# Expert stage of a convolution and attention network: tiles of 128 tokens, chunks of 256 and a last chunk of 64

## The reference, cut to what matters

```python
def _L2_ffn_ref(x, norm_w, wq, keys, expert_down, expert_up):
    HEADS = 8; DIM_KEY = 32; K = 16; NUM_KEYS = 64
    ...
    q = (x_norm @ wq).reshape(B, T, HEADS, 2, DIM_KEY)
    sim = jnp.einsum('bthpd,hkpd->pbthk', q, keys)
    s1, i1 = jax.lax.top_k(sim[0], K)
    s2, i2 = jax.lax.top_k(sim[1], K)
    all_idx = (i1[..., :, None] * NUM_KEYS + i2[..., None, :]).reshape(B, T, HEADS, K * K)
    all_scores = (s1[..., :, None] + s2[..., None, :]).reshape(B, T, HEADS, K * K)
    final_scores, pk = jax.lax.top_k(all_scores, K)
    final_idx = jnp.take_along_axis(all_idx, pk, axis=-1)
    wd = expert_down[final_idx]
    wu = expert_up[final_idx]
    hidden = jnp.einsum('btd,bthkd->bthk', x_norm, wd)
    hidden = jax.nn.gelu(hidden, approximate=False)
    hidden = hidden * jax.nn.relu(final_scores)
    return jnp.einsum('bthk,bthkd->btd', hidden, wu)
```

## Time and profile before

| | before |
|---|---|
| median of 3 executions | 2701.39 us |
| profiled execution, its own time | 2689.78 us |
| its span | 2688.1 us |
| PE busy, PEld busy | 2236.6, 1940.0 us |
| DVE busy | 1847.0 us |
| ACT, POOL busy | 663.9, 435.8 us |
| mean granted clock of TensorE | 0.82 of full speed |
| all data moved by DMA | 107.85 MB |

### The profile page before, as it was taken

The page is one execution under the profiler, slowest core; times in us unless marked ns, Lnnn a source line. Parts: engine busy times, 40 slices in busy tenths (PEclk is TensorE's granted clock), DMA queues, the critical chain, the costliest instruction groups (busy, mean ns, idle before and its releaser), DMA issues. The chain is left out here.

```text
span 2688.1 us, 50156 instructions
## 1 busy us (share of the span) xinstructions
PE 2236.6 (83%) x18017; PEld 1940.0 (72%) x18017; DVE 1847.0 (69%) x7732; ACT 663.9 (25%) x1527; POOL 435.8 (16%) x521
## 2 busy tenths in 40 slices
PE   6585999955989889989989889989888799648994
PEld 3464788734889788888989889889888577326663
DVE  4334666448889889898898898898895577440003
ACT  1432455432211111211211211111111255402220
POOL 2003444310101201102102012012012310030003
PEclk8777999966788697787787887887786799869996
DMA  1104444225000000000000000000000233042323
GB/s 53 34 18 98 106 108 99 47 73 118 5 4 1 5 5 2 5 5 2 5 1 5 5 1 5 5 1 5 1 1 1 65 83 81 7 165 82 104 92 102
DMA packets 87043, 107.85 MB, mean 40 GB/s; under 512 B 26222, under 2 KB 75502, under 8 KB 86062
## 3 DMA queue, kind: packets, MB, share of 16 engines
q1 hardware_dynamic: 81328, 96.62, 13.7%
q0 software_dynamic: 3296, 6.43, 0.9%
q10 hardware_dynamic: 2176, 1.61, 0.2%
HBM read 70.61 MB, written 30.51 MB: 38 GB/s over the span
## 5 line engine op out<-in xcount | busy, mean ns | idle before, releaser
L1540 PE MATMUL peer_x_ps<-peer_oh_h,peer_oh_a 128*128 128x32 bf16 x3136 | 417.2, 249 | 6.1 <-DVE peer_oh_l L1812 4.4
L1540 PEld LDWEIGHTS peer_x_ps<-peer_oh_h,peer_oh_a 128*128 128x128 bf16 x3136 | 414.2, 149 | 8.5 <-DVE peer_oh_l L1812 5.7
L1541 PE MATMUL peer_x_ps<-peer_oh_l,peer_oh_a 128*128 128x32 bf16 x3136 | 417.8, 249 | 0.0
L1541 PEld LDWEIGHTS peer_x_ps<-peer_oh_l,peer_oh_a 128*128 128x128 bf16 x3136 | 412.9, 149 | 3.6 <-issue 1.5
L1516 PE MATMUL peer_x_ps<-peer_xc,peer_dt 128*128 128x224 f32 x1792 | 374.4, 373 | 31.7 <-DMA peer_up<-in_L_ffn_expert_up_dram 19.4
L1482 POOL TENSOR_TENSOR peer_g<-peer_g,peer_qt 128x448 f32<-128x448 f32 x112 | 189.7, 1715 | 1275.0 <-ACT peer_qt L1639 1274.9
L1550 PE MATMUL peer_out_ps<-peer_g,peer_up 128*128 128x224 f32 x1792 | 370.9, 372 | 30.6 <-issue 28.4
L1516 PEld LDWEIGHTS peer_x_ps<-peer_xc,peer_dt 128*128 128x128 f32 x1792 | 362.1, 204 | 40.0 <-issue 34.6
L1550 PEld LDWEIGHTS peer_out_ps<-peer_g,peer_up 128*128 128x128 f32 x1792 | 361.1, 203 | 37.6 <-issue 32.4
L1617 ACT ACTIVATE peer_g<-peer_x_ps 128x448 f32<-128x448 f32 x224 | 121.9, 544 | 652.1 <-PE peer_x_ps L1516 652.1
L1277 DVE TENSOR_REDUCE l_attn_mx<-l_attn_s_ps 98x4 f32<-98x392 f32 (+1 forms) x320 | 175.0, 560 | 140.4 <-PE l_attn_s_ps L1047 100.6
(11 more groups left out here) (308 smaller groups left out, 3633.5 us busy)
## 6 DMA issues: line engine op xcount, KB each, us to landing
moe_w<-in_L_ffn_w_dram SPq DMA_DIRECT2D x16, 1024.0 KB, 9.1
l_attn_pieces_q_dram<-l_attn_pieces_q SPq DMA_DIRECT2D x16, 294.0 KB, 3.9
l_attn_pieces_k_dram<-l_attn_pieces_k SPq DMA_DIRECT2D x16, 294.0 KB, 3.1
l_attn_stq<-l_attn_pieces_q_dram SPq DMA_DIRECT2D x16, 294.0 KB
l_attn_stk<-l_attn_pieces_k_dram SPq DMA_DIRECT2D x16, 294.0 KB
peer_g<-n_L_ffn_expert_down_dram SPq DMA_DIRECT2D x8, 512.0 KB, 6.7
peer_up<-in_L_ffn_expert_up_dram SPq DMA_DIRECT2D x2, 2048.0 KB
l_xi<-net_x SPq DMA_DIRECT2D x16, 196.0 KB, 2.3
```

Source lines behind the costliest of these rows:

```text
L1540: nc.tensor.matmul(x_ps[q][:, i * J:(i + 1) * J], oh_a[hb % 2][:, :, t], oh_h[hb % 2][:, :, t], start=True, stop=False)
L1541: mm = nc.tensor.matmul(x_ps[q][:, i * J:(i + 1) * J], oh_a[hb % 2][:, :, t], oh_l[hb % 2][:, :, t], start=False, stop=True)
```

## The change

`TT` becomes 128 and with it `CT` 256, `HT` 64 and `GT` 16. 3136 tokens are 12 chunks of 256 and a rest of 64, half a tile. Every helper gets the number of tokens (`cols`, `rows`, `now`) as an argument; the rest is a thirteenth chunk with one tile, one quarter and 8 of the 16 lists in the second selection. The hardware loop now covers chunks 2 to 9; 10, 11 and the rest are written out behind it. SyncE gets one more load, of 64 tokens. Eleven intermediates of `make_codes` lose their own space and are put behind the tables in the `oh_a` buffers; for that the wait for `m_done` moves from L1749 to the top of `make_codes`, ahead of the candidate sums. Elements per partition of the steps in `make_codes` and `top_halves` stay what they were.

```diff
-    TT = 112
+    TT = 128
...
+    REST = NT - NCHUNK * CT
+    assert REST == HT
...
-        i16f, step16 = S.sb("i16f", [TT, NTILE * G16, TOP]), S.sb("step16", [TT, 2, TOP, HH], BF16)
...
-        sel = [oh_a[p][0:TT, :, :].rearrange("t r k -> t (r k)")[:, 0:TOP * PP].rearrange("t (a k) -> t a k", a=TOP) for p in range(2)]
+        flat = [oh_a[p][0:TT, :, :].rearrange("t r k -> t (r k)") for p in range(2)]
+        sel = [flat[p][:, 0:TOP * PP].rearrange("t (a k) -> t a k", a=TOP) for p in range(2)]
+
+        def behind(p, word, words, dt):
+
+            o = TOP * PP + 2 * word
+            return flat[p][:, o:o + 2 * words].bitcast(dt)
+
+        t1, t2, t3 = (behind(0, i * PP, PP, F32) for i in range(3))
+        bits, col = behind(0, 3 * PP, PP, U32), behind(0, 4 * PP, PP, U32)
...
             for p in range(2):
-                chunk(NCHUNK - 2 + p, p, p == 1)
+                chunk(NCHUNK - 2 + p, p, CT, CT if p == 0 else REST)
+            chunk(NCHUNK, 0, REST, 0)
+
+        def tile_rows(tokens):
+
+            return [min(TT, tokens - t0) for t0 in range(0, tokens, TT)]
...
             steps(sp, NCHUNK // 2 - 1, body)
+            sp.wait_ge(h_done, NPAIR * (NCHUNK - 1))
+            sp.dma_start(xc[0][:, :, 0:REST], xn_dram[:, :, NCHUNK * CT:NT].rearrange("k p t -> p k t")).then_inc(xc_in[0], 16)
...
-                            mm = nc.tensor.matmul(x_ps[b][:, jj * CT:(jj + 1) * CT], dt[:, k, 2 * jp + jj, :], xc[p][:, k, :],
+                            mm = nc.tensor.matmul(x_ps[b][:, jj * CT:jj * CT + cols], dt[:, k, 2 * jp + jj, :], xc[p][:, k, 0:cols],
...
-            def chunk(n, p, last):
-                hidden(n, p, range(EARLY))
-                for t in range(NTILE):
-                    turn(n, t)
-                hidden(n, p, range(EARLY, NPAIR))
-                if not last:
-                    queries(n + 1, 1 - p)
-                for hb in range(NHB):
+            def chunk(n, p, now, then):
+                hidden(n, p, range(EARLY), now)
+                for t, rows in enumerate(tile_rows(now)):
+                    turn(n, t, rows)
+                hidden(n, p, range(EARLY, NPAIR), now)
+                if then > 0:
+                    queries(n + 1, 1 - p, then)
+                next_rows = tile_rows(then)
+                for hb in range(now // HT):
                     scatter(n, hb)
-                    if hb < NTILE and not last:
-                        scores(n + 1, hb)
-                experts_out(n)
+                    if hb < len(next_rows):
+                        scores(n + 1, hb, next_rows[hb])
+                experts_out(n, now)
...
-            def make_codes(n):
-
+            def make_codes(n, tiles):
+
+                heads, rows = len(tiles) * NH, tiles[0]
                 v = v16[:, :, :].rearrange("t (h w) a -> t w h a", w=2)
                 o = 0
                 chain.wait()
+                wait(dve, m_done, 4 * NHB * n)
...
-                top16(f16, p16, [cv[:, h, :] for h in range(HH)])
+                top16(f16[0:rows, 0:heads, :], p16[0:rows, 0:heads, :], [cv[0:rows, h, :] for h in range(heads)])
...
-                wait(dve, m_done, 4 * NHB * n)
...
-            def chunk(n, p, last):
-                if p == 0:
+            def chunk(n, p, now, then):
+                if p == 0 and now == CT:
                     chain.turn(n, 2)
...
-                for hb in range(NHB - 1):
-                    one_hots(n, hb + 1)
+                for hb in range(n_hb):
+                    if hb + 1 < n_hb:
+                        one_hots(n, hb + 1)
                     if hb < LATE:
                         weigh(n, hb)
-                if not last:
-                    for t in range(NTILE):
-                        top_halves(n + 1, t)
-                    make_codes(n + 1)
+                if then > 0:
+                    for t, rows in enumerate(tile_rows(then)):
+                        top_halves(n + 1, t, rows)
+                    make_codes(n + 1, tile_rows(then))
                 dve.wait_ge(out_done, n + 1)
-                xs = x[:, :, bass.ds(n * CT, CT)]
+                xs = x[:, :, bass.ds(n * CT, now)]
```

More of the change, by code:

```diff
@@ L1474, in _ @@
             nc.gpsimd.memset(keys_b[:, :, :], 0.0).then_inc(iota_done, 1)
-            def chunk(n, p, last):
-                for hb in range(LATE, NHB):
+            def chunk(n, p, now, then):
+                for hb in range(LATE, now // HT):
                     for q in range(4):
@@ L1502, in scores, with hidden @@
                 for m in range(4):
-                    mm = nc.tensor.matmul(sim_ps[m // 2][0:TT, (m % 2) * 4 * NK:(m % 2 + 1) * 4 * NK], qt[:, m, t * TT:(t + 1) * TT],
+                    mm = nc.tensor.matmul(sim_ps[m // 2][0:rows, (m % 2) * 4 * NK:(m % 2 + 1) * 4 * NK], qt[:, m, t * TT:t * TT + rows],
                                           keys_b[:, m, :], start=True, stop=True)
                 mm.then_inc(sim_done, 1)
-            def hidden(n, p, pairs):
+            def hidden(n, p, pairs, cols):
                 for jp in pairs:
@@ L1558, in _ @@
             pe.wait_ge(keys_ready, 1)
-            queries(0, 0)
+            queries(0, 0, CT)
             for t in range(NTILE):
-                scores(0, t)
+                scores(0, t, TT)
             for s in range(J // JS):
@@ L1618, in hidden_out, with chunk @@
                                          ACT.Gelu).then_inc(gelu_done, 1)
-            def chunk(n, p, last):
+            def chunk(n, p, now, then):
                 wait(act, out_done, n)
-                hidden_out(n, range(EARLY))
-                for t in range(NTILE):
+                hidden_out(n, range(EARLY), now)
+                for t, rows in enumerate(tile_rows(now)):
                     act.wait_ge(tr_done, NTILE * n + t + 1)
-                    ts = slice(t * TT, (t + 1) * TT)
+                    ts = slice(t * TT, t * TT + rows)
@@ L1636, in chunk @@
-                for k in range(4 * (NHB - LATE)):
+                    nc.scalar.activation(wh_t[:, ts], tr_ps[:, 2 * TT:2 * TT + rows], ACT.Copy)
+                    nc.scalar.activation(a_t[:, ts], tr_ps[:, 0:rows], ACT.Copy)
+                    nc.scalar.activation(b_t[:, ts], tr_ps[:, TT:TT + rows], ACT.Copy).then_inc(tr_ready, 1)
+                hidden_out(n, range(EARLY, NPAIR), now)
+                if then > 0:
+                    query_out(n + 1, then)
+                    for t, rows in enumerate(tile_rows(then)):
+                        score_out(n + 1, t, rows)
@@ L1637, in chunk @@
+                for k in range(4 * max(0, now // HT - LATE)):
                     act.wait_ge(m_done, 4 * NHB * n + 4 * LATE + k + 1)
@@ L1702, in fold, with top_halves @@
                 else:
-                    chain.step(nc.vector.tensor_tensor(out[:, :], m[:, 0, :], m[:, 1, :], ALU.add))
-            def top_halves(n, t):
+                    chain.step(nc.vector.tensor_tensor(out, m[:, 0, :], m[:, 1, :], ALU.add))
+            def top_halves(n, t, rows):
                 dve.wait_ge(sim_ready, NTILE * n + t + 1)
@@ L1823, in _, with chunk @@
             for t in range(NTILE):
-                top_halves(0, t)
-            make_codes(0)
-            def chunk(n, p, last):
-                if p == 0:
+                top_halves(0, t, TT)
+            make_codes(0, tile_rows(CT))
+            def chunk(n, p, now, then):
+                if p == 0 and now == CT:
                     chain.turn(n, 2)
-                low_weights(n, 0)
+                tiles, n_hb = tile_rows(now), now // HT
+                low_weights(n, 0, tiles[0])
                 one_hots(n, 0)
-                low_weights(n, 1)
-                for hb in range(NHB - 1):
-                    one_hots(n, hb + 1)
+                if len(tiles) > 1:
+                    low_weights(n, 1, tiles[1])
+                for hb in range(n_hb):
+                    if hb + 1 < n_hb:
+                        one_hots(n, hb + 1)
                     if hb < LATE:
                         weigh(n, hb)
-                if not last:
-                    for t in range(NTILE):
-                        top_halves(n + 1, t)
-                    make_codes(n + 1)
+                if then > 0:
+                    for t, rows in enumerate(tile_rows(then)):
+                        top_halves(n + 1, t, rows)
+                    make_codes(n + 1, tile_rows(then))
                 dve.wait_ge(out_done, n + 1)
-                xs = x[:, :, bass.ds(n * CT, CT)]
-                nc.vector.tensor_tensor(xs, xs, out_ps[:, 0:KC * CT].rearrange("p (k t) -> p k t", k=KC), ALU.add).then_inc(x_done, 1)
+                xs = x[:, :, bass.ds(n * CT, now)]
+                nc.vector.tensor_tensor(xs, xs, out_ps[:, 0:KC * CT].rearrange("p (k t) -> p k t", k=KC)[:, :, 0:now], ALU.add).then_inc(x_done, 1)
             chunks(dve, chunk)
```

98 lines of the change are left out of this document (47 added, 51 removed).

## The result

The changed kernel takes **2795.36 us** (median of 4 runs, 2789.94 to 2806.3), the one before 2699.99 on the same chip (4 runs, 2695.79 to 2703.5): a ratio of 1.037, 95% interval 1.034 to 1.039. 2598 was forecast, with 0.04 for slower. The profiled execution took 2789.94 us, its span is 2788.2.

The account below looks back on a forecast made before the run. VectorE, in a loop through TensorE, was taken as the bound. First scatter 693.3 + intervals 1184.7 + last chunk 114.1 = 1992.1 us stage end, -103.0: 2586.8 profiled, plus 11.6 gives 2598 us; range 2575 to 2642.

Parts of the forecast that it names:

- What grows by 8/7 in a full chunk: Token-dependent work on VectorE's path per full chunk: scatters 0 and 1 14.7 to 16.8 us, one-hots 8.3 to 9.2.
- PE's sum: TensorE's own time per full chunk: 105.2 us, with scatters 33.7, some 2 us behind VectorE's path.
- Slower: the scatter's operands: Scatter matmuls reading one-hots at 128 bytes fetch slower; 16 ns more each eats the gain, up to 2955 us; chance 0.05.
- The fixed part: VectorE's selection and codes stay 60.1 us per chunk on 128 partitions, 11 times between chunks instead of 13.
- No gain: the fixed part isn't fixed: Selection and codes on VectorE grow by 8/7, 60.1 to 68.7 us, giving 2693 us; chance 0.03.
- The interval: Time between first scatters of successive full chunks: 107.7 us mean, 11 times, 1184.7 us, VectorE the bound by a hair.
- TensorE takes over: Low clock makes TensorE bound the chunks, mean 110 us, +25, 2623 us; chance 0.20 shared with the costly last chunk.
- POOL beside the one-hots: In a full chunk, POOL's products may hold a second VectorE one-hot instruction for 0 to 1.3 us; 1.0 taken.
- The start: Before the chunk loop: longer first hidden pairs move the first scatter from 690.01 to 693.3 us.
- The last chunk: The final 64 tokens: 114.1 us from the preceding chunk's scatter 0 to the stage's end, narrow hidden and output records at 120 ns.
- Dear tail: In the 64-token chunk, 208 narrow records cost 230 ns each: +23, 2621 us; chance 0.20 shared with TensorE bounding.
- The moved wait: VectorE's wait for all the chunk's scatters, ahead of the code steps: no waiting time, cost 0.

Follow-up runs that it names:

- the repaired kernel: Changed kernel with rows of all three one-hot buffers 136 bytes apart instead of 128, codes sharing the space of v16 and i16: 2597.63 us, ratio 0.961 to before.
- the fourth experiment: Kernel before (tiles of 112), one-hot rows in buffer 1 at 128 bytes, buffer 0 at 112, codes in the space of v16 and i16: 2747.5 us, one run.

## Why the prediction was wrong, step by step

- **The step that failed** is "What grows by 8/7 in a full chunk. Scatters 0 and 1: 14.7 to 16.8", and with it "scatters ... 33.7" in PE's sum. It took 66 ns per matmul over into a layout with another step. Measured: 2 x 12.6 = 25.2, and about 50 for four. In place of it stands the rival "Slower: the scatter's operands", mechanism and price: break-even was put at 16 ns more per matmul, and 32 more came (98 against 66): 6272 x 32 ns = 201 us against a gain of 103 makes +98, measured +100.1 in the span. All matmuls lie on the path because TensorE became the bound: VectorE waits 13 us in the chunk shown.
- **Its chance** of 0.05 rested on two sentences. "Both steps are far apart in memory" is true and beside the point: 32 bytes is near and 136 farther, and both are good. "Nothing in the trace depends on a step" was no evidence against: the trace of before has one single step, 112 bytes, for these loads, so it could not show a dependence. That argument speaks for a wide bound, such as this part asked of unknown costs everywhere else, and the range left the bound out.
- **The fixed part** held: 60.2 us for 60.1, on 128 partitions. Sixteen MAX8 take 2.16 us (1079.87 to 1082.03; 2.12 in the earlier trace rows), and the 128x2048 product 1215 to 1217 where 1223 was worked out. "No gain: the fixed part isn't fixed" is refuted.
- **The interval.** With the scatter repaired (136 bytes) it is (1859.05 - 681.89) / 11 = 107.0 us, forecast 107.7. But the bound is mostly the other engine than I had "by a hair": in nine of twelve chunks TensorE reaches the first turn without a wait, in three it waits 0.8 to 1.7 us for the codes, where 1 to 2 were forecast for all. By its rows: scatters and scores 40.5, POOL's last product 2.4, output 29.9, ten pairs 17.3, turns 2.1, six pairs and queries 13.8 = 106.0, and in three chunks the pause at a loop start, 2.1 to 2.9. The forecast for TensorE was 105.2. The low clock that the idling had caused left the pairs, as forecast: 10.53 us for 48 matmuls with 256 columns, where the earlier trace rows has 10.49 with 224. The rival "TensorE takes over" had the right engine and a mean that its own terms don't give: eight intervals of 108.1 and three of 110.7 make 108.8, not 110, so +12 and not +25. TensorE took over at 107.0.
- **POOL beside the one-hots**: one instruction of a chunk is held, as before: the last product of the fourth set takes 2.65 us in the repaired kernel at 1029.90, all others 1.22 or 1.23. The second hold, for which 1.0 us was added, is there in two chunks (the first, and the set at 1674.17) and missing in nine; in the last full chunk three are held, see the last chunk below. In the chunk of the changed kernel shown above there is none at all: its last set ends at 1079.95, and POOL's first product starts at 1078.90 and takes the delay itself (2.60 us).
- **The start**: from the first hidden product to the first scatter 32.5 us before, 34.9 after; +3.3 was forecast, +2.4 came.
- **The last chunk** was mis-sized: 128.4 us in the repaired kernel instead of 114.1. Hidden with 64 columns took 9.0 us for 80 records (113 ns; 120 taken), the output product 27.57 for 128, **215 ns each** instead of 120: +12.2. The stretches above show why: hidden runs at a granted clock of 1.00 (2.4 GHz), the output product at 0.50 (1.2 GHz) from its first microsecond to its last, with TensorE busy throughout; behind the wait of 3.4 us for the one-hots and the scatter the clock doesn't come back before the stage ends. The sum had 1.7 us for low clock. So the upper bound of 230 ns was the right price for 128 of the 208 records, a good half of the rival "Dear tail" (+23). The one-hots for the fourth scatter of the chunk before came 4.3 us late, too, a wait that the sum of TensorE's times left out. Three instructions of that set are held beside POOL, for 3.9 us together (DVE, then PE):

```profile
1884.57 2.63 DVE L1833 TENSOR_TENSOR peer_oh_l<-peer_b_t,peer_iota_f 128x2048 bf16<-128x2048 bf16 x1
1887.23 2.45 DVE L1836 TENSOR_TENSOR peer_oh_h<-peer_oh_l,peer_wh_t 128x2048 bf16<-128x2048 bf16 x1
1889.61 2.51 DVE L1836 TENSOR_TENSOR peer_oh_l<-peer_oh_l,peer_wl_t 128x2048 bf16<-128x2048 bf16 x1
```

```profile
1892.17 0.27 PE L1561 MATMUL peer_x_ps<-peer_oh_h,peer_oh_a 128*128 128x32 bf16 x1 [4.25 <-DVE peer_oh_l L1836]
```

- **The 2597.6 of the repaired kernel against 2598** is better than its terms, and luck. Against the forecast for a profiled execution the first scatter came 11.4 us earlier (681.89 for 693.3), the intervals took 7.5 less, the last chunk 14.3 more and what follows 15.1 more, +10.5 together; and of the 11.6 that were added to get from the profiled execution to the median, 0.3 came.
- **The moved wait, and the temporaries in the one-hot buffers**, taken at nothing: between the set's last product and the selection no wait is to be seen, and ahead of the codes the changed kernel has 0.2 us in the whole stage. No run undoes them by themselves.
- "What follows starts from there and is not touched": from the last output matmul to the end of the span there were 593 us before, 607 in the changed kernel and 605 to 608 in its variants (618 in the one with 2 bytes). But the fourth experiment, which has the tiles of before, has 605 as well, so the new tile isn't what makes it; that the other stages differ so much between executions is likely (the profile of before is of an execution 10 us under its median), but not shown. The entry to this stage, the first hidden product, lies between 639 and 658 us in the profiles, likewise.

## What to carry to other kernels

A tile size can also be the row length of an operand, and then it sets the step at which another engine reads it; a matmul's price measured at another step is then no price, and the unknown belongs into the range with both ends. Pad the rows of a strided stationary operand, or block them, so that the step isn't 64 or 128 bytes (other multiples of 32 above 32 weren't run): here 8 bytes more per row turned +3.7% into -4%. Of two busy engines, one that shows as 100% busy in both kernels can still work at two thirds of the pace: count instructions in a window.

## What was not expected of the hardware

- Loading 128 bf16 columns from a step of 128 bytes costs 32 to 36 ns more per matmul with 32 moving columns than from 112, 132, 136 or 144, in stretches whose granted clock is 0.50 to 0.68; 64 bytes costs 14 more, at 0.87. That the stationary operand makes most of it is shown (8.12 against 11.55 us in one program, with 8 ns left for the moving ones). Why is not. The Trainium skill (SBUF — State Buffer, Door 1: The DMA port swizzle) says that memory lines are 16 bytes long and that each access on a new line pays; the 58 ns at 2 bytes against 62 at 16 agrees, but by it 16, 112, 128 and 136 bytes would cost the same, and 98 against 65 ns does not agree.
- The Trainium skill (TensorE: Matmul & The Clock Gate, Weight-path perf modes — Fast Weight Load (FWL) and DoubleRow) has a load of 128 bf16 weights split into four chunks of 32 columns, read side by side. By the layouts the chunks lie 4096 bytes apart at a step of 128, 2048 at 64, 4352 at 136, so that four readers on one part of the memory would fit the table; so would neighbouring columns that fall on one part. No run here tells them apart: every kernel here reads the stationary operand with one step, so the distance of the chunks changes only with it, and it stays open.
- The granted clock stayed at 0.50 for all 27.6 us of the last output product, with TensorE at 100% busy: busy is no promise of the higher clock.
